# Count blocks of a graph kernel: turned by TensorE and evicted by VectorE, or turned by a DMA transpose

## What is computed

```python
summed = jax.ops.segment_sum(x[src], dst, num_segments=n)
deg = jax.ops.segment_sum(jnp.ones_like(src, dtype=x.dtype), dst, num_segments=n)
agg = summed / jnp.maximum(deg, 1.0)[:, None]
out = agg @ W_l.T + b_l + x @ W_r.T          # L0; L1, L2 and L3 are of the same kind
```

## Time and profile before

| | us |
|---|---|
| median of 3 runs | 732.84 (732.76 to 733.78) |
| span of the profiled execution | 731.7 |
| TensorE matmul busy | 706.2 (97%) |
| VectorE busy | 433.6 (59%) |
| ScalarE busy | 303.6 (41%) |
| GpSimd busy | 31.0 (4%) |

### The profile page before, as it was taken

The page is one execution under the profiler, slowest core; times in us unless marked ns, Lnnn a source line. Parts: engine busy times, 40 slices in busy tenths (PEclk is TensorE's granted clock), DMA queues, the critical chain, the costliest instruction groups (busy, mean ns, idle before and its releaser), DMA issues.

```text
span 731.7 us, 11918 instructions
## 1 busy us (share of the span) xinstructions
PE 706.2 (97%) x3435; PEld 551.0 (75%) x3436; DVE 433.6 (59%) x853; ACT 303.6 (41%) x613; POOL 31.0 (4%) x34
## 2 busy tenths in 40 slices
PE   3989999999999999999999999999999899999997
PEld 1545666688788888888888888888887678887786
DVE  5998999865456744422333466655699962247333
ACT  3887988522334222365311343222544352223321
POOL 1010111100000000000000000000222000000000
PEclk9999999999999999999999999999999999999999
DMA  7000000100012000011000201000200000000011
GB/s 245 5 1 15 20 24 30 57 0 0 2 59 73 0 0 1 6 69 58 0 0 1 74 4 54 1 0 0 74 0 0 2 2 0 1 0 0 32 57 54
DMA packets 12851, 18.68 MB, mean 26 GB/s; under 512 B 652, under 2 KB 5060, under 8 KB 12808
## 3 DMA queue, kind: packets, MB, share of 16 engines
q1 hardware_dynamic: 10472, 15.04, 6.3%
q10 hardware_dynamic: 2336, 3.08, 1.2%
HBM read 15.57 MB, written 2.56 MB: 25 GB/s over the span
## 4 chain that ended last, share of the span: by engine, by line
PE 78%; DVE 3%; issue 2%; ACT 1%; DVEq 0%; ACTq 0%
PE ps L1119 36%; PE ps L1161 36%; PE ps L1107 3%; PE ps L1063 2%; ACT cstage L485 1%; PE ps L1038 1%; PE ps L1022 0%; DVE own L890 0%; DVE countT L692 0%; DVE own L862 0%; DVE stats L658 0%; DVE own L795 0%; ACT apart L417 0%; DVE hT_lo L735 0%; DVE z L722 0%
## 5 line engine op out<-in xcount | busy, mean ns | idle before, releaser
L1161 PE MATMUL ps<-p_hi,cstage 128*128 128x512 f32 x600 | 234.5, 391 | 3.7 <-ACT cstage L485 2.0
L1161 PE MATMUL ps<-p_lo,cstage 128*128 128x512 f32 x600 | 233.6, 389 | 0.0
L1119 PE MATMUL ps<-w_hi,hT_hi 128*128 128x512 f32 x400 | 161.3, 403 | 2.1 <-DVE hT_lo L735 1.9
L1119 PE MATMUL ps<-w_hi,hT_lo 128*128 128x512 f32 x400 | 156.5, 391 | 0.0
L1119 PE MATMUL ps<-w_lo,hT_hi 128*128 128x512 f32 x400 | 156.0, 390 | 0.0
L1161 PEld LDWEIGHTS ps<-p_hi,cstage 128*128 128x128 f32 x600 | 112.6, 188 | 28.5 <-issue 5.3
L1161 PEld LDWEIGHTS ps<-p_lo,cstage 128*128 128x128 f32 x600 | 112.7, 188 | 23.1
L862 DVE SCALAR_TENSOR_TENSOR own<-ps,nodal,own 128x512 f32 (+1 forms) x60 | 44.9, 749 | 120.2 <-PE ps L1161 119.9
L1063 PE MATMUL ps<-src_hot,dst_hot 128*128 128x512 bf16 (+1 forms) x576 | 107.2, 345 | 6.3 <-DVE src_hot L675 5.4
L675 DVE TENSOR_SCALAR src_hot<-iota,nodeT 128x1250 bf16<-128x1250 f16 x192 | 94.2, 552 | 11.5 <-PE ps L1063 8.2
L485 ACT CAST cstage<-countT 128x1280 fp32r (+1 forms) x50 | 62.6, 1263 | 85.5 <-PE ps L1161 85.4
(11 more groups left out here) (124 smaller groups left out, 507.1 us busy)
## 6 DMA issues: line engine op xcount, KB each, us to landing
x<-in_x ACTq DMA_DIRECT2D x1, 2304.0 KB
out_x<-x SPq DMA_DIRECT2D x9, 256.0 KB
wstage<-in_L_gnn_W SPq DMA_DIRECT2D x2, 1024.0 KB, 5.2
vec<-in_L_gnn_b SPq DMA_DIRECT2D x4, 256.0 KB, 5.3
wstage<-in_L_gnn_W_r SPq DMA_DIRECT2D x4, 256.0 KB, 2.8
wstage<-in_L_gnn_W1l SPq DMA_DIRECT2D x1, 1024.0 KB, 5.1
wstage<-in_L_gnn_W1r SPq DMA_DIRECT2D x1, 1024.0 KB, 5.4
wstage<-in_L_gnn_W2l SPq DMA_DIRECT2D x1, 1024.0 KB, 5.3
```

The source lines that it names most:

```text
L1119: last = nc.tensor.matmul(ps[:, bank + r, :], a[:, r, k, :], w[:, slot, k, :], start=n == 0, stop=n == len(pairs) - 1)
L1161: last = nc.tensor.matmul(ps[:, AGG + r, :], cstage[:, part, k, :], p_[:, k, :], start=n == 1, stop=n == 2 * len(parts) * NT)
```

## The change

ScalarE's L402 writes the counts straight into `count16` as 16-bit numbers, with the degrees summed as before. `cblock`, GpSimd's copies, TensorE's turns of counts (L1038) and VectorE's evictions (L692) are gone. For each block SP issues one DMA transpose from `count16[:, b, :]` into the 128 columns of `countT16` that belong to the block. On SP's queue transpose b stands ahead of chunk load b + 2. A semaphore `first_split` now keeps the shared bank of `turn_first` in order: TensorE's turn of chunk b waits until VectorE has finished `w_lo` of the chunk before. ScalarE and GpSimd wait for all ten transposes where they waited for `cT_out`.

```diff
-    cblock, _ = place("cblock", [P, 2, NP], F32, place.end)
...
+    def wait_turned_counts(engine):
+        engine.wait_ge(cT_loaded, 16 * NT)
...
-            order = [("v", r) for r in rows[:5]] + [("c", c) for c in range(2, 2 * KF)] + loads[:3]
+            order = [("v", r) for r in rows[:5]]
+            for b in range(NT):
+                order += [("t", b)] + ([("c", b + 2)] if b + 2 < 2 * KF else [])
+            order += loads[:3]
...
+                if kind == "t":
+
+                    sp.wait_ge(counts_out, what + 3)
+                    sp.dma_start_transpose(countT16[:, :, what * P:(what + 1) * P], count16[:, what, :]
+                                           ).then_inc(cT_loaded, 16)
+                elif kind == "c":
...
-            pool.sem_inc(c16_done, 2)
-            with pool.Fori(0, NT - 1, 2) as b0:
-                for par in range(2):
-                    pool.wait_ge(counts_out, b0 + par + 3)
-                    nc.gpsimd.tensor_copy(count16[:, bass.ds(b0 + par, 1), :],
-                                          cblock[:, par, :]).then_inc(c16_done, 1)
-            pool.wait_ge(cT_out, 3 * NT + 3)
+            pool.wait_ge(counts_out, NT + 2)
+            wait_turned_counts(pool)
...
-                act.wait_ge(c16_done, b + 1)
-                nc.scalar.activation(cblock[:, par, :], ps[:, 3 * par:3 * par + 3, :].rearrange("p a b -> p (a b)")[:, 0:NP],
+                nc.scalar.activation(count16[:, bass.ds(b, 1), :],
+                                     ps[:, 3 * par:3 * par + 3, :].rearrange("p a b -> p (a b)")[:, 0:NP],
                                      ACT.Copy, accum_out=deg_in[:, bass.ds(b, 1)]).then_inc(counts_out, 1)
...
-            act.wait_ge(c16_done, NT + 2)
-            act.wait_ge(cT_out, 3 * NT + 3)
+            act.wait_ge(counts_out, NT + 2)
+            wait_turned_counts(act)
...
+                dve.wait_ge(wlo_done, KF * n + c + 1)
+                dve.sem_inc(first_split, 1)
...
-                        visits = first_givers(b0 + k + 1)
-                        turned_out(b0 + k - 1, GROUPS[:2])
-                        later_givers(b0 + k + 1, *visits)
-
+                        later_givers(b0 + k + 1, *first_givers(b0 + k + 1))
                         split_first(w, b0 + k - blocks[0])
-                        turned_out(b0 + k - 1, GROUPS[2:])
-            turned_out(NT - 2, GROUPS)
             lo(L0, 0, 0)
-            turned_out(NT - 1, GROUPS)
...
-                pe.wait_ge(cT_out, 3 * b + 5)
+                pe.wait_ge(first_split, b + 1)
...
-                    turn_counts(turned, par, GROUPS[2:])
                     turn_first(turned, par)
...
-                    turn_counts(b0 + k - 1, k, GROUPS[:2])
                     count(b0 + k + 1, k, turned=b0 + k - 1)
-            turn_counts(NT - 2, 0, GROUPS[:2])
...
             turn(L0, 0, 0)
-            turn_counts(NT - 2, 0, GROUPS[2:])
-            turn_counts(NT - 1, 1, GROUPS)
```

More of the change, by code:

```diff
@@ L164, in gnn_kernel @@
     apart_done, nodes_placed = sem("apart_done"), sem("nodes_placed")
-    counts_ready, counts_out, cT_ready, cT_out, c16_done = (
-        sem("counts_ready"), sem("counts_out"), sem("cT_ready"), sem("cT_out"), sem("c16_done"))
+    counts_ready, counts_out, cT_loaded = sem("counts_ready"), sem("counts_out"), sem("cT_loaded")
     vec_loaded = [sem(f"vec{k}_loaded") for k in range(5)]
@@ L177, in gnn_kernel @@
     chunk_loaded = [sem(f"chunk{k}_loaded") for k in range(2)]
+    first_split = sem("first_split")
     coarse_set, exact_set, fine_set = sem("coarse_set"), sem("exact_set"), sem("fine_set")
@@ L225, in visits_of @@
         return nc.s_assert_within(t0, 0, ET - 1), nc.s_assert_within(t1, 2 * RING, ET + 2 * RING - 1), shift
-    assert 8 < NT <= 12
-    GROUPS = range(3)
     def dma_rows(engine, dram, sbuf, sem_, store=False):
@@ L263, in _ @@
             for kind, what in order:
-                if kind == "c":
+                if kind == "t":
[3 more added lines that the diff above has]
+                elif kind == "c":
                     sp.wait_ge(wT_ready, what - 1)
@@ L579, in _ @@
         def _(dve):
+            dve.sem_inc(first_split, 1)
             for s_ in (z_ready, lo_done, plo_done, q_done, t_done, sum_done):
                 dve.sem_inc(s_, 2)
-            dve.sem_inc(cT_out, 3)
             nc.vector.memset(e_int[:, :, 1, :], NOWHERE).then_inc(pads_set, 1)
@@ L685, in later_givers @@
                     givers(b, t, shift)
[L687 to L694, removed]
             EARLY = NT - 3
@@ L769, in _ @@
             nc.vector.tensor_tensor(dis2[:, :], dis[:, :], dis[:, :], ALU.mult).then_inc(scale_step, 1)
-            dve.wait_ge(c16_done, NT + 2)
             dve.wait_ge(scale_step, 3)
@@ L1139, in _ @@
                     pe.wait_ge(top_done, 1)
-                    pe.wait_ge(cT_out, 3 * NT + 3)
                     nc.tensor.transpose(ps[0:1, AGG, 0:P], top[:, 0:1], ident[:, :]).then_inc(top_turned, 1)
```

## The result

The changed kernel takes 741.0 us (740.1 to 741.4, four runs) where the kernel before takes 732.82 beside it: a ratio of 1.0109, interval 1.0094 to 1.0123. It is slower by 8 us; 729.2 was forecast, and the range ended at 734. The profiled execution spans 738.4 us, with a granted clock of 0.995, where before spans 731.7 at 1.000.

A forecast was written before the change was run, and what follows sets the result against it. The counting stage was taken as doubly bound, ScalarE and TensorE both needing about 8.2 us per two-group block, with only TensorE relieved. 732.84 less 3.9 gained plus 0.3 for a late landing gave 729.2, range 727 to 734.

The forecast's parts named there:

- Term (a): Counting blocks of three groups, 60 to 95 us: ScalarE's waits for slots that TensorE frees vanish, 1.3 us gained.
- Term (b): Counting blocks of two groups: ScalarE's pace stays, but TensorE no longer trails it in the last block, 0.86 us gained.
- Term (c): Tail from last count to first L0 product: 2.93 us in place of 4.66, 1.73 us gained.
- the sum: Counting stage and hand-over to L0: 3.9 us gained, last count at 135.1 and first product at 138.0.
- The term of 0.3 us for a late landing: Before ScalarE's L0 loop: last transpose lands after 5.3 us, free up to 5.0 after the last counts, so 0.3 lost.
- Rivals 1 and 2: DMA transposes land slowly but keep up, 731.4 to 734, chance 0.12; or the rings back up, 751 or 805, chance 0.15.
- VectorE's new wait for its own w_lo: Counting blocks: only the next block's first src_hot is queued behind it, at most 0.1 us, counted as nothing.
- The room of 2 us: Counting blocks: without evictions VectorE needs about 6 us a block, so it has 2 us spare and bounds nothing.
- which nobody feels: SP's queue in the counting stage: transposes one to six are issued up to a block late, at no cost.
- from there on the chain is TensorE back to back, and I move it as a block: From the first L0 product at 141.95 us on: everything later shifts by as much as that product starts earlier.
- the clock: TensorE idling about 1 us a block in the counting stage leaves its granted clock unchanged; nothing put on it.
- Rival 4: ScalarE pays for 16-bit output or TensorE stalls at block starts: 2.5 to 4 us of gain lost, 731.4 to 733, chance 0.05.

The follow-up runs named there:

- the variant with both edits: Changed kernel with asserted bounds moved, VectorE's wait for its own w_lo removed and 80 never-run TensorE instructions added: 729.37 us, ratio 0.9956 to the kernel before.
- after: The changed kernel as built, nothing else altered, against the kernel before: 741.0 us, ratio 1.0109.
- the variant with padding: Changed kernel with asserted bounds moved and 80 never-run instructions in TensorE's branch for large counts, VectorE's wait kept: 732.9 us, ratio 1.0005 to the kernel before.
- the first eight instructions: Changed kernel with only asserted bounds moved, which lengthens TensorE's program by 8 instructions: 737.67 us, ratio 1.0075 to the kernel before.
- the other eighty: 80 never-run semaphore increments in TensorE's branch for large counts, added to the changed kernel with moved bounds: 732.9 us, ratio 1.0005 to the kernel before.
- the shifted kernel before: Kernel before with moved bounds and 160 never-run instructions in TensorE's branch for large counts, nothing of the change: 742.6 us, ratio 1.0141 to the kernel before.

## Why the prediction was wrong, point by point

**Right: removals, tail, landing.** With the two faults out, the kernel takes 729.4, against 729.2 forecast. ScalarE's blocks start 7.9 to 8.5 us apart there, as its own pace was forecast. Term (a), 1.3 us: at the last block of three groups the variant with both edits is 1.71 us ahead (94.48 against 96.19), 0.48 of it from its first block on, so 1.23. Term (b), 0.86: over the blocks of two groups it gains 0.58. Term (c), 1.73: 2.91 in place of 4.66, 1.75. The first product is 4.04 us earlier, of which 0.48 were there from the start; the sum was 3.9. That the sum fits so well is in part luck: VectorE, said to bound nothing, is still what TensorE waits for most (5.9 us against 1.8 for ScalarE), and the longer register loads were in no term. The output of ScalarE cost nothing, as said.

**Right, too cautious: the transpose.** 3.8 us to the landing where I took 5.3. The term of 0.3 us for a late landing is nothing. The issue is 1.35 us where I had 0.37 for a load and added 3.3 for ten squares. Rivals 1 and 2 did not happen: the trace has no transpose that anyone waited for. Against the 1309 ns per 128x128 of the Trainium skill (VectorE: DVE Perf Modes, "The three transpose paths") stand ten squares for each issue, 1.54 us apart when back to back. The other rule of the Trainium skill that I weighed (Advanced Engine Details and Errata, "X-Bar Transpose (TRN2)"), "as fast as regular DMAs", is the nearer: 3.8 us for 320 KB, against 2.9 for a load of 256 KB.

**Wrong: "VectorE's new wait for its own w_lo has the next block's first src_hot queued behind it; at most the overlap of two instructions, 0.1 us".** This step failed first. What is queued behind the wait is not src_hot alone but the load and bounds of three registers (1.7 us in the chain above, from 120.56 to 122.27), which until then ran beside w_lo and an eviction. It cost 2.8 to 3.5 us of the run. I had read the same loads as ScalarE's floor of 0.8 to 1.3 us a block, and did not ask what hid them on VectorE. The room of 2 us was real, but the gap grew from 1.50 to 3.34 us, and TensorE came to wait up to 1.8 us a block.

**Wrong: transposes one to six are issued late, "which nobody feels".** They have a price that no term held: register loads of VectorE and ScalarE beside them take up to 1 us longer. In the counting stage of single executions this came to 0.4 us with the transposes spread over it, hardly more than two such executions differ by, and to 1.8 with eight of them back to back.

**Wrong: "from there on the chain is TensorE back to back, and I move it as a block".** The block does not move rigidly: removing instructions shifts where branch targets lie. From after to the variant with padding the time fell by 8.1 us (3.3 with the first eight instructions, 4.8 with the other eighty), more than all that the change could bring. No rival had it.

**Wrong: the clock.** I put nothing on it because TensorE had idled a sixth of a stretch at 1.00. In the counting stage that held. Behind stalls of 1.7 to 2.95 us in after it fell to 0.88 and 0.90, and 180 matmuls took 1.7 us more. These runs give no rule for it: in the shifted kernel before a stall of 3.35 us left it at 1.00 and the later one brought 0.83.

**Rival 4**, that TensorE meets another stall at the block's start, named the right place for the first fault, and its size too: with the padding, and so with that fault alone, the kernel takes 732.9, inside the rival's 731.4 to 733. But I gave it 0.05, and the second fault came on top.

## What to carry to other kernels

A wait of an engine for its own result is priced by what its sequencer has behind it: look for register loads, bounds and a loop's turn, and put them ahead of the wait, or let those who need the result wait for its semaphore themselves. An edit that adds or removes instructions on an engine with taken branches is compared only after the code behind has been shifted back to where it lay; otherwise some us belong to the placement. If a stage far behind the edit has a new idle time called issue at the start of a branch, pad first and explain afterwards. Where an engine loads registers in every block, look at the length of these loads once DMA transposes run beside them.

## What the runs showed of the hardware

- Eight instructions more in TensorE's program move the time by 3.3 us, and 160 that never run put 8.8 us on the kernel before.
- A stall of TensorE is paid twice where the clock falls: 12.4 us of standing brought 0.68 as the mean clock of the 20 us around.
- VectorE's src_hot takes 1.54 us in place of 0.55 beside a GpSimd copy of 1.25 us. In the kernel before these copies fell mostly beside VectorE's reads of PSUM, and cost little.
- A register load of three numbers takes 0.74 to 0.77 us on VectorE, and up to 1.67 when it begins 0.6 to 2.5 us after the issue of a DMA transpose; on ScalarE it is 0.69 to 0.72, and up to 1.77.
- A DMA transpose of ten squares, 320 KB, holds its queue's engine 1.35 us and lands after 3.8 us, where a load of 256 KB lands after 2.9.
